# First stage of a transformer block: the first batch of x in two halves, two ropes back to back, layer-norm statistics spread over the feed-forward rounds

## The reference

```python
xn = _layernorm(x, axis=-1)            # (x - mean) / sqrt(var + 1e-5)
x = x + attn(xn, Wq, Wk, Wv, Wo) + ffn(xn, w_gate, w_up, w_down)
# attn: 16 query heads of 64, keys and values made of 8 heads
xq, xk, xv = rope(q @ Wq), rope(kv @ Wk), kv @ Wv      # xk, xv repeated to 16 heads
scores = softmax(xq @ xk * scale); out = (scores @ xv) @ Wo
# ffn: integer weights times 1/127, hidden width 384
h = silu(x @ w_gate.T) * (x @ w_up.T); return h @ w_down.T
```

## Time and profile before

| | |
|---|---|
| Median of 3 runs | 1128.86 us (1128.25 to 1129.79) |
| Profiled execution, its own time | 1127.29 us |
| Its span, first to last instruction | 1125.4 us |
| Busy share of the span | PE 97%, DVE 81%, POOL 76%, ACT 64% |
| Chain that ended last | PE 93%, DVE 4%, ACT 2%, DMA 1% |
| Mean granted clock of TensorE | 0.991 of full speed |

### The profile page before, as it was taken

One profiled execution on the slowest core, in us unless ns is written; L12 is line 12 of the kernel. 1 busy time (PEld: TensorE's weight loads), 2 busy tenths in 40 slices (PEclk: granted clock), 3 DMA queues, 4 the chain that ended last, 5 costly groups with the idle time before them and its releaser, 6 DMA issues.

```text
span 1125.4 us, 17086 instructions
## 1 busy us (share of the span) xinstructions
PE 1090.5 (97%) x6288; PEld 661.9 (59%) x6288; DVE 912.1 (81%) x1023; ACT 722.1 (64%) x1327; POOL 853.3 (76%) x268
## 2 busy tenths in 40 slices
PE   5899999999999999999999999999999999999987
PEld 4787455666656565656656565656666565654533
DVE  7686878888888888888888888888888888887755
ACT  3333666666666676667666676667666676666664
POOL 3321878888888888888888888888888888888770
PEclk9899999999999999999999999999999999999998
DMA  6662907144260817154260817153260817140000
GB/s 238 159 246 101 269 1 196 38 150 121 48 186 2 232 38 205 29 142 129 50 183 2 232 38 205 29 155 117 51 183 2 232 38 202 32 109 26 4 2 19
DMA packets 56338, 124.98 MB, mean 111 GB/s; under 512 B 8000, under 2 KB 19520, under 8 KB 54080
## 3 DMA queue, kind: packets, MB, share of 16 engines
q1 hardware_dynamic: 56256, 123.90, 37.8%
HBM read 53.08 MB, written 10.49 MB: 56 GB/s over the span
## 4 chain that ended last, share of the span: by engine, by line
PE 93%; DVE 4%; ACT 2%; DMA 1%; issue 1%; ACTq 0%; DVEq 0%
PE bank_s L553 24%; PE scores L392 22%; PE bank_o L407 21%; PE scores L374 8%; PE bank_m L382 3%; PE bank_m L417 3%; PE bank_m L420 2%; PE bank_m L443 2%; PE scores L493 2%; PE bank_s L510 1%; PE bank_m L427 1%; PE bank_m L434 1%; DVE row_max L950 1%; PE bank_o L510 1%; PE bank_m L510 1%
## 5 line engine op out<-in xcount | busy, mean ns | idle before, releaser
L871 ACT ACTIVATE prob<-bank_s 128x512 f32<-128x512 f32 x992 | 566.2, 599 | 274.0 <-PE bank_s L553 263.9
L950 DVE TENSOR_REDUCE row_max<-scores 128x1 f32<-128x1024 f32 x512 | 601.2, 1215 | 97.0 <-PE scores L392 92.9
L1181 POOL TENSOR_TENSOR prob_sum<-prob_sum,prob 128x2048 f32<-128x2048 f32 x93 | 427.1, 4592 | 13.4
L553 PE MATMUL bank_s<-qk_pack 98*128 98x512 f32 x992 | 393.4, 427 | 3.4 <-ACT prob L871 2.0
L392 PE MATMUL scores<-qk_pack 96*128 96x512 f32 x1024 | 323.4, 402 | 2.4 <-DVE rope L945 1.7
L553 PEld LDWEIGHTS bank_s<-qk_pack 98*128 98x128 f32 x992 | 178.2, 188 | 176.2 <-ACT prob L871 117.5
L407 PE MATMUL bank_o<-prob,v 128*32 128x512 f32 x2048 | 254.4, 603 | 0.0
L392 PEld LDWEIGHTS scores<-qk_pack 96*128 96x128 f32 x1024 | 184.6, 189 | 61.1 <-DVE row_max L950 28.8
L1181 POOL TENSOR_TENSOR prob_sum<-prob_sum,prob_pair 128x2048 f32<-128x2048 f32 x31 | 142.5, 4596 | 80.9 <-DVE prob_pair L1043 80.9
L1173 POOL TENSOR_TENSOR prob_sum<-prob 128x2048 f32<-128x2048 f32 x31 | 142.2, 4587 | 0.0
L1125 POOL TENSOR_TENSOR qk_stage<-rope,qk_stage 128x512 fp32r<-128x512 f32 x64 | 81.8, 1280 | 77.9 <-ACT qk_stage L757 77.8
(11 more groups left out here) (105 smaller groups left out, 754.3 us busy)
## 6 DMA issues: line engine op xcount, KB each, us to landing
qk_pack<-qk_stage SPq DMA_DIRECT2D x384, 128.0 KB, 4.5
table<-tables SPq DMA_DIRECT2D x16, 2048.0 KB, 9.7
w_stage<-w_scratch SPq DMA_DIRECT2D x14, 640.0 KB, 4.7
v<-v_stage SPq DMA_DIRECT2D x32, 256.0 KB, 7.4
xT_scratch<-xT_hl SPq DMA_DIRECT2D x4, 1024.0 KB, 9.2
x_stage<-xT_scratch SPq DMA_DIRECT2D x4, 1024.0 KB, 6.6
w_scratch<-w_split SPq DMA_DIRECT2D x1, 2560.0 KB, 15.1
x_all<-x SPq DMA_DIRECT2D x4, 512.0 KB, 11.7
```

Source lines behind the costliest of these rows:

```text
L553: mm(bank_s[:, h % 2, :], qk_pack[j][0:SCORE_K, 1, kt // QT, h, (kt % QT) * 128:(kt % QT + 1) * 128], qk_pack[j][0:SCORE_K, 0, t, h, :], s ...
L871: A(prob[:, kt % RING, h, :], bank_s[:, h % 2, :], ACT.Exp).then_inc(prob_ready, 1)
L950: V.tensor_reduce(row_max[:, m:m + 1], scores[:, at:at + 2, :].rearrange("p c k -> p (c k)"), axis=AX.X, op=ALU.max).then_inc(max_read, 1)
L1181: TT(prob_sum[:, t], prob_sum[:, t], part, ALU.add).then_inc(sum_done, 1)
```

## The change

The loads of batch 0 and of the attention weights are cut in two, so that half a batch and the weights of group 0 come first. Statistics go by five groups: the two halves of batch 0, then one for each later batch. `statistics` becomes `moments` (the `bn_stats`) and `inverse_root` (all behind it). For batches 1 to 3, `moments` and `inverse_root` are put into the rounds of the feed-forward loop (`MOMENTS_AT`, `ROOT_AT`), and the root is no longer taken by ScalarE: VectorE forms a first guess from the bits of the number in one operation and makes three Newton steps of four operations. Unit 0 is projected before chunk 1 is transposed; the first half of unit 1's rope stands right behind unit 0's rope, the second half behind `hidden` of round 0; `down(0)` goes to round 2, where `down(1)` follows it. Chunk 2 is normalised in round 4 and transposed in round 5, one round later than before. ScalarE rounds the weights of groups 2 and 3 behind `stage_v` of unit 0.

```diff
-GROUPS = [slice(0, KT), slice(KT, NT)]
+GROUPS = [slice(0, QT), slice(QT, KT), slice(KT, 2 * KT), slice(2 * KT, 3 * KT), slice(3 * KT, NT)]
+GROUP_OF = [0, 1, 2, 2, 3, 3, 4, 4]
+MOMENTS_AT = {2: range(KT, 2 * KT), 4: range(2 * KT, 2 * KT + QT), 5: range(2 * KT + QT, 3 * KT), 11: range(3 * KT, NT)}
+ROOT_AT = {3: 2, 7: 3, 12: 4}
-TRANSPOSE_AT = {HT * c - 2: c for c in range(2, CHUNKS)}
+TRANSPOSE_AT = {HT * c - (1 if c == 2 else 2): c for c in range(2, CHUNKS)}
...
@@ SyncE @@
-            sp.dma_start(x_all[:, 0:KT, :], x[0].rearrange("(n p) d -> p n d", p=128)).then_inc(x0_in, 16)
-            sp.dma_start(ident[:], ident_in).then_inc(w_in, 16)
-            sp.dma_start(w_raw[:].rearrange("p g c m -> p g (c m)"), w_qkv.rearrange("g p n -> p g n")).then_inc(w_in, 16)
+            x_first = x[0].rearrange("(n p) d -> p n d", p=128)
+            sp.dma_start(x_all[:, 0:QT, :], x_first[:, 0:QT, :]).then_inc(x0_in, 16)
+            sp.dma_start(ident[:], ident_in).then_inc(ident_loaded, 16)
+            sp.dma_start(w_raw[:, 0].rearrange("p c m -> p (c m)"), w_qkv[0]).then_inc(w_in, 16)
+            sp.dma_start(x_all[:, QT:KT, :], x_first[:, QT:KT, :]).then_inc(x0_rest, 16)
+            sp.dma_start(w_raw[:, 1:G].rearrange("p g c m -> p g (c m)"), w_qkv[1:G].rearrange("g p n -> p g n")).then_inc(w_rest, 16)
...
@@ TensorE @@
-            pe.wait_ge(w_in, 32)
-            for n in range(2):
-                transpose_x(n)
+            pe.wait_ge(ident_loaded, 16)
+            transpose_x(0)
+            pe.wait_ge(xT_hi, 1)
+            pe.wait_ge(xT_lo, 1)
+            pe.wait_ge(w_hi, 1)
+            pe.wait_ge(w_lo, 1)
+            project_early(0)
+            transpose_x(1)
+            project_v_early(0)
             pe.wait_ge(xT_hi, 2)
             pe.wait_ge(xT_lo, 2)
-            pe.wait_ge(w_hi, 1)
-            pe.wait_ge(w_lo, 1)
-            for w in range(2):
-                project_early(w)
-                project_v_early(w)
+            project_early(1)
+            project_v_early(1)
...
-                if n > 0:
+                if n == 2:
+                    pe.wait_ge(rope_read, 4 * half + 4)
+                    down(0)
+                    down(1)
+                elif n > 2:
                     pe.wait_ge(rope_read, 4 * half + 4)
                     down(n - 1)
...
@@ ScalarE @@
             root(0)
-            act.wait_ge(w_in, 32)
+            round_x(0)
+            act.wait_ge(w_in, 16)
             round_w(0)
-            for n in range(2):
-                round_x(n)
+            root(1)
+            act.wait_ge(w_rest, 16)
+            round_w(1)
             act.wait_ge(gu_f, 1)
             nc.scalar.copy(wgu[:, 0], wgu_f).then_inc(gu_hi, 1)
-            for g in range(1, G):
+            round_x(1)
+            stage_v(0, 0, 0)
+            for g in range(2, G):
                 round_w(g)
-            stage_v(0, 0, 0)
             for c in range(2):
                 round_hi(c, 0, 0, 0)
             stage_v(1, 1, 0)
-            root(1)
...
@@ VectorE @@
+            def refine(k, n, last):
+                tiles = GROUPS[k]
+                dve.wait_ge(newton, n)
                 V.tensor_tensor(rstd[:, 3, tiles], rstd[:, 2, tiles], rstd[:, 2, tiles], ALU.mult).then_inc(newton, 1)
...
+            def inverse_root(k):
+                tiles = GROUPS[k]
+                variance(k)
+                if k < 2:
+                    dve.wait_ge(sqrt_done, k + 1)
+                    V.reciprocal(rstd[:, 2, tiles], rstd[:, 1, tiles]).then_inc(newton, 1)
+                    refine(k, 4 * k + 1, True)
+                else:
+                    dve.wait_ge(var_done, k + 1)
+                    V.tensor_scalar(rstd[:, 2, tiles].bitcast(I32), rstd[:, 0, tiles].bitcast(I32), -0.5, float(0x5F3759DF),
+                                    ALU.mult, ALU.add).then_inc(newton, 1)
+                    for i in range(3):
+                        refine(k, 8 + 12 * (k - 2) + 4 * i + 1, i == 2)
...
             dve.wait_ge(x0_in, 16)
-            statistics(0)
+            moments(range(0, QT))
+            inverse_root(0)
             normalise_x(0)
+            dve.wait_ge(x0_rest, 16)
+            moments(range(QT, KT))
+            low_x(0)
+            low_w(0)
+            inverse_root(1)
             normalise_x(1)
-            low_w(0)
-            for n in range(2):
-                low_x(n)
...
+            low_x(1)
             rotate(0, 0, 0)
-            dve.wait_ge(x_in, 16 * (B - 1))
-            statistics(1)
+            rotate(1, 1, 0, range(0, 1))
...
-                if n == 1:
-                    rotate(1, 1, 0)
+                if n == 0:
+                    rotate(1, 1, 0, range(1, 2))
...
+                if n == 2:
+                    dve.wait_ge(x_in, 16 * (B - 1))
+                if n in MOMENTS_AT:
+                    moments(MOMENTS_AT[n])
+                if n in ROOT_AT:
+                    inverse_root(ROOT_AT[n])
                 if n + 1 in TRANSPOSE_AT:
                     normalise_x(TRANSPOSE_AT[n + 1])
```

More of the change, by code:

```diff
@@ L153, in build @@
         where = [bank_o, bank_s[:, 0, :]] + (CHUNKS - 2) * [scores[:, 2, :]]
+        ident_loaded, w_rest, x0_rest = sem("ident_loaded"), sem("w_rest"), sem("x0_rest")
         x0_in, x_in, w_in, ffn_in, wo_loaded = sem("x0_in"), sem("x_in"), sem("w_in"), sem("ffn_in"), sem("wo_loaded")
@@ L933, in _, with rotate @@
             V = nc.vector
-            def rotate(w, t, s):
+            def rotate(w, t, s, halves=range(2)):
                 at_least(dve, lo_done, 2 * w)
                 dve.wait_ge(table_in, 16 * (s + 1))
-                for k in range(2):
+                for k in halves:
                     dve.wait_ge(proj_ready, 5 * w + 2 * k + 1)
@@ L960, in _, with moments, variance @@
             V.memset(ones[:], 1.0).then_inc(filled, 1)
-            def statistics(k):
+            def moments(tiles):
+                for n in tiles:
+                    V.bn_stats(stats[:, n, :], x_all[:, n, :]).then_inc(stats_done, 1)
+            def variance(k):
                 tiles = GROUPS[k]
-                for n in range(tiles.start, tiles.stop):
-                    V.bn_stats(stats[:, n, :], x_all[:, n, :]).then_inc(stats_done, 1)
                 for n in range(tiles.start, tiles.stop):
@@ L970, in statistics @@
                 V.tensor_scalar(rstd[:, 0, tiles], mean_var[:, tiles, 1], EPS, None, ALU.add).then_inc(var_done, 1)
-                dve.wait_ge(sqrt_done, k + 1)
-                V.reciprocal(rstd[:, 2, tiles], rstd[:, 1, tiles]).then_inc(newton, 1)
-                dve.wait_ge(newton, 4 * k + 1)
+            def refine(k, n, last):
+                tiles = GROUPS[k]
+                dve.wait_ge(newton, n)
                 V.tensor_tensor(rstd[:, 3, tiles], rstd[:, 2, tiles], rstd[:, 2, tiles], ALU.mult).then_inc(newton, 1)
-                dve.wait_ge(newton, 4 * k + 2)
+                dve.wait_ge(newton, n + 1)
                 V.tensor_tensor(rstd[:, 1, tiles], rstd[:, 3, tiles], rstd[:, 0, tiles], ALU.mult).then_inc(newton, 1)
-                dve.wait_ge(newton, 4 * k + 3)
+                dve.wait_ge(newton, n + 2)
                 V.tensor_scalar(rstd[:, 3, tiles], rstd[:, 1, tiles], -0.5, 1.5, ALU.mult, ALU.add).then_inc(newton, 1)
-                dve.wait_ge(newton, 4 * k + 4)
-                V.tensor_tensor(rstd[:, 1, tiles], rstd[:, 2, tiles], rstd[:, 3, tiles], ALU.mult).then_inc(rstd_done, 1)
+                dve.wait_ge(newton, n + 3)
+                if last:
+                    V.tensor_tensor(rstd[:, 1, tiles], rstd[:, 2, tiles], rstd[:, 3, tiles], ALU.mult).then_inc(rstd_done, 1)
+                else:
+                    V.tensor_tensor(rstd[:, 2, tiles], rstd[:, 2, tiles], rstd[:, 3, tiles], ALU.mult).then_inc(newton, 1)
+            def inverse_root(k):
[5 more added lines that the diff above has]
+                    refine(k, 4 * k + 1, True)
+                else:
+                    dve.wait_ge(var_done, k + 1)
[3 more added lines that the diff above has]
+                        refine(k, 8 + 12 * (k - 2) + 4 * i + 1, i == 2)
             def normalise_x(c):
-                dve.wait_ge(rstd_done, min(c // 2, 1) + 1)
+                dve.wait_ge(rstd_done, GROUP_OF[c] + 1)
                 if c >= 4:
```

## The result

The changed kernel takes 1138.09 us (median of 13 executions, 1135.96 to 1141.42) against 1129.09 (13 executions, 1127.93 to 1135.23): ratio 1.0072, 95% interval 1.0057 to 1.0087; the quotient of the two medians, 1.0080, lies inside it. The forecast was 1134.3, its own range 1131.3 to 1137, and 1127.5 to 1139 with the rivals. The profiled execution of after has a span of 1138.1 us and a mean granted clock of 0.983.

What follows compares the result with a forecast made beforehand. TensorE bounds the kernel, but the untouched main stage leaves only the first stage's end to move: -5.5 + 4.9 + 2.9 + 0.7 + 2.35 = +5.4 on 1128.9 gives 1134.3 us, range 1131.3 to 1137, with rivals 1127.5 to 1139.

Steps and rivals of the forecast that it cites:

- the lower clock: Rival: TensorE falls to its lower level in new waits near rounds 6, 9, 13; 2.35 us lost once, 1136.7; chance 0.18.
- Ahead of the loop: From first load to `hidden(2)`: smaller first load and fewer early statistics bring it to 31.95 from 37.49, D = -5.5.
- the bound given: Unit 0's projection, twelve matmuls ahead of the loop: 4.5 us taken, with up to +0.9 as bound.
- no tile waits for the packing DMAs: Rounds 2 to 5: packing DMAs start 2.7 us earlier; head 0 is packed at 39.3, needed at 42.
- The root and GpSimd's hold: Rounds 2 to 5: GpSimd's fill and first addition hold batch 1's root by 1.2 us, bounds 0 to 2.4.
- the hold on the wrong operation: Ahead of the loop: GpSimd's weight subtraction slows `normalise_x(1)`, as an addition once made it 2.19 instead of 1.11 us.
- Rounds 6 to 13: VectorE's roots and statistics delay TensorE: D from -0.6 to +2.3 by round 9, +5.4 at round 13's transposes.
- all three named places: TensorE waits near 2.5 us: gates of rounds 6 and 9 for `low_x`, round 13's transposes for `normalise_x(5)`.
- the sizes come smaller: Rival: GpSimd holds nothing, `normalise_x` of rounds 6 and 9 meets no addition; D = +1.5, 1130.4 us; chance 0.18.
- one sign of being wrong: Rounds 7, 8 or 13: VectorE idle there was listed among the signs that the forecast is wrong.
- Runs beside TensorE: Rival: VectorE's new work runs beside TensorE in the rounds; D = -3.3, 1125.6 us; chance 0.14.
- I see no reason: Main stage: no reason seen for it to become longer or shorter itself; the change does not touch it.

Runs made afterwards that it cites:

- the run with the later fill: Changed kernel, but GpSimd fills `qk_pack` only when `normalise_x(2)` is over: 1134.8 us, ratio 1.0054 to the kernel before.
- the version that uses it: Changed kernel with batch 1's statistics before the second rope, later roots on GpSimd, chunk 2 in round 4, fill behind it: 1127.69 us (0.9990), again 1126.82 (0.9971).
- its warmed variant: The version with batch 1's statistics in the gap, plus spare matmuls around the first transposes and before unit 1's projection: 1128.3 us (14 and 16), 1127.36 (8 and 4).

## Why the prediction was right, and which terms were too small

The direction was right, and so was the path: up to the transposes of round 13 every milestone came within 1.4 us of the forecast. The time, 1138.09, lies above the forecast's own range and inside only the one that its rivals widened; what it had given as a rival, the lower clock, came on top of its sum.

- **Ahead of the loop**, forecast D = -5.5, measured -5.17. The order of events is as told: the second rope is held by GpSimd until 25.3. That the number is so close is in part luck. Unit 0's projection began 0.5 us earlier than forecast (10.89 instead of 11.4) and took 1.0 longer (5.46 instead of 4.5, inside the bound given); and unit 1's, partly at the lower clock, brought `hidden(0)` 0.5 late. In the run with the later fill, without that fall, `hidden(2)` came at 31.09, 0.9 ahead of the forecast. That no tile waits for the packing DMAs was wrong: the tile of round 5 waited 1.25 us for them at 40.14. It cost nothing there, since TensorE then waited for VectorE anyway.
- **The root and GpSimd's hold** is the mis-sized term: 1.2 us forecast, bounds 0 to 2.4, measured 1.94; from `hidden(2)` to the gate of round 6 it was 13.8 us instead of 13.3. The fill, which reads nothing from SBUF, held a one-input scaling (L990, 1.11 us) and let the aggregation at 35.07 through; the addition, which reads SBUF, held a product of two SBUF inputs (L996, 1.17 us). The Trainium skill ("SBUF — State Buffer", section "SBUF: two separate sides") had it: the port pair that VectorE shares with GpSimd is locked for a whole instruction, against `tensor_scalar` in a mode that takes both ports, and against an operation with two SBUF inputs only while GpSimd reads SBUF. The measurement agrees, and the run with the later fill shows the two holds gone; a small product beside a fill alone stands in no run. At `normalise_x(1)` the forecast had the hold on the wrong operation: L1003, a product, took 1.41 us, and the normalising itself went free.
- **Rounds 6 to 13.** Forecast increments +2.9, then +3.1 to the transposes of round 13; measured +3.47 and +2.65. Small operations at 0.17 us, 0.20 apart, and waits of TensorE at all three named places: right. In the first increment two things cancel that its sum did not have: `normalise_x(3)` missed the addition and took 1.11 us (50.16) instead of 2.19 before, and VectorE waited 0.92 us ahead of `hidden(7)` (52.19), behind TensorE at its lower clock. So one piece of "the sizes come smaller" came, and so did one sign of being wrong, VectorE idle in round 7, without moving the sum. With two Newton steps less, the stretch from the gate of round 6 to the transposes of round 13 lost 2.4 us on before instead of 6.1, so the work was on the path. "Runs beside TensorE" is out, and "the sizes come smaller" as a whole.
- **The clock**, given 0.18 as a rival of its own, came in addition. Behind round 6 it is 0.53 over 3 us, at most 1.4 us lost; behind round 13 it adds most of the 1.56 us between the transposes and the first score, for which the forecast had nothing. That the waits cause it is argued, not shown: in the rounds of after the falls stand behind the waits of 2.43 and 2.19 us and not behind that of 1.45, but with one Newton step a wait of 2.40 us ahead of round 6 brought none. Nor is the loss as a whole the clock's: the one execution of after with a mean clock of 0.991 took 1136.08 us, and those of before with 0.991 on three chips 1126.7 to 1131.8.
- **The main stage.** "I see no reason" was wrong for the profiled execution, 4.8 us longer with 14 us at the lower level. It is not the change's doing alone: main stages of 1015.6 to 1023.4 us stand in the profiles of this study, with falls at other times in each. The medians lie 9.0 us apart; if the first stage is as long in every execution as in the profiled one, about 1 us of that lies behind the first score. What decides where the clock falls in an execution stays open.

## What to carry to other kernels

Before work is moved off a wait and into a loop, count the free time of the engine that gets it, round by round: here VectorE had 3 us free in 23 and was given 5 per batch, and the gain of 5 us ahead of the loop went into it. A gap that the new order itself opens (here 3.2 us behind the first rope) is the place for such work, and the version that uses it is the only one, with its warmed variant, for which a whole interval lay below the kernel before, by 0.3% and in one of its two series. Look at what GpSimd starts beside a chain of small VectorE operations: a fill and an addition at the wrong time cost more than the chain (4.2 against 2.8 us, in the run with the root on GpSimd).

## What the hardware showed that was not expected

- A fill of only 2 partitions by 4096 on GpSimd, 3.5 us, held VectorE's scalings: four of 128x128 took 5.26 us instead of 1.11 when it and an addition stood beside them, and one of 8 columns took 1.11 us instead of 0.17. The aggregation beside it took its usual 0.64 us.
- Small dependent operations on GpSimd are not much slower than on VectorE: 0.20 us each and 0.28 apart, against 0.17 and 0.20.
- At the start, with 3.8 us and 1.1 us of spare matmuls ahead of it, unit 0's projection took 3.00 us; without them, in the same series, 5.26. The granted-clock column reads 1.00 in that stretch in both cases; there only the durations show the level.
